# Cross-attention with a gated residual, first batch: banks of the gate products, places of two memory splits, of the query's split and of the weight clusters, and the ragged tile stacked

## The reference

```
mp    = memory @ W_mem.T                       # 1601 x 512
attn  = softmax(x @ mp.T / sqrt(512))          # 512 x 1601
ctx   = attn @ mp                              # 512 x 512
gate  = sigmoid([x, ctx] @ W_gate.T + b_gate)
fused = x + gate * ctx
out   = fused * rsqrt(mean(fused**2) + 1e-6) * norm_w
```

## Time and profile before

| | |
|---|---|
| median of 3 runs | 537.66 us (537.37 to 537.76) |
| the profiled execution | 537.72 us, of which the span is 535.9 us |
| TensorE's granted clock, mean | 0.996 |
| busy, share of the span | PE 98%, DVE 90%, ACT 60%, POOL 32% |
| the chain of waits | PE 93%, DVE 4%, the rest 1% or less each |

### The profile page before, as it was taken

How to read it: one execution, slowest core, us unless ns; L and a number is a source line. 1 busy time by engine, 2 the same in 40 slices (tenths; PEclk the granted TensorE clock), 3 DMA queues, 4 the chain that set the end, 5 groups by cost and what they waited for, 6 DMA issues and landing times.

```text
span 535.9 us, 8824 instructions
## 1 busy us (share of the span) xinstructions
PE 524.8 (98%) x2364; PEld 431.7 (81%) x2364; DVE 482.8 (90%) x797; ACT 323.2 (60%) x614; POOL 172.2 (32%) x129
## 2 busy tenths in 40 slices
PE   8998999999999999999999999999999999999994
PEld 7876888888888888888888888888888888888883
DVE  3799958999799998999989998899979999899967
ACT  4675636676467655686465863666557765558524
POOL 0004610185004740066200950027400573008702
PEclk9999999999999999999999999999999999999998
DMA  9967263511687027840378105870267502401033
GB/s 226 269 122 125 64 102 91 100 40 31 181 164 130 20 59 168 177 81 20 112 149 185 39 20 173 148 144 21 75 153 167 110 20 76 141 31 39 2 117 119
DMA packets 186118, 56.38 MB, mean 105 GB/s; under 512 B 161756, under 2 KB 175592, under 8 KB 186100
## 3 DMA queue, kind: packets, MB, share of 16 engines
q1 hardware_dynamic: 185572, 55.64, 44.7%
q10 hardware_dynamic: 528, 0.52, 0.3%
HBM read 46.15 MB, written 8.39 MB: 102 GB/s over the span
## 4 chain that ended last, share of the span: by engine, by line
PE 93%; DVE 4%; DMA 1%; issue 1%; ACT 1%; SPq 0%; POOLq 0%; POOL 0%; DVEq 0%
PE bank L391 22%; PE bank L393 21%; PE bank L392 21%; PE bank L567 8%; PE bank L568 8%; PE bank L569 8%; PE bank L470 1%; DMA mem_raw<-in_ctx_dram 1%; PE bank L551 1%; PE bank L550 1%; PE bank L603 0%; DVE wg1t_lo L904 0%; DVE p_lo L904 0%; DVE fused L1081 0%; SPq L339 0%
## 5 line engine op out<-in xcount | busy, mean ns | idle before, releaser
L1256 POOL TENSOR_TENSOR psum_rows<-psum_rows,p_tmp 128x512 f32<-128x512 f32 (+1 forms) x88 | 129.6, 1473 | 39.5 <-ACT p_tmp L735 36.1
L904 DVE TENSOR_TENSOR p_lo<-p_tmp,p_hi 128x512 fp32r<-128x512 f32 (+1 forms) x104 | 89.2, 858 | 5.9 <-ACT p_hi L696 5.9
L1267 POOL TENSOR_TENSOR fused<-fused,x_again 128x512 f32<-128x512 f32 x14 | 17.9, 1300 | 219.1 <-DVE fused L1077 219.1
L391 PE MATMUL bank<-q_hi,mt_hi 128*128 128x512 f32 (+1 forms) x208 | 81.9, 394 | 0.0
L393 PE MATMUL bank<-q_hi,mt_lo 128*128 128x512 f32 (+1 forms) x208 | 81.3, 391 | 0.0
L392 PE MATMUL bank<-q_lo,mt_hi 128*128 128x512 f32 (+1 forms) x208 | 81.2, 390 | 0.0
L735 ACT ACTIVATE p_tmp<-s 128x512 f32<-128x512 f32 (+1 forms) x104 | 64.4, 626 | 27.6 <-DVE s L968 26.5
L567 PE MATMUL bank<-p_hi,mem_hi 128*128 128x512 f32 (+1 forms) x196 | 76.4, 390 | 0.0
L568 PE MATMUL bank<-p_lo,mem_hi 128*128 128x512 f32 (+1 forms) x196 | 76.3, 390 | 0.0
L569 PE MATMUL bank<-p_hi,mem_lo 128*128 128x512 f32 (+1 forms) x196 | 76.3, 389 | 0.0
L696 ACT ACTIVATE s<-bank 128x512 f32<-128x512 f32 (+1 forms) x104 | 62.0, 596 | 19.1 <-PE bank L393 18.7
(11 more groups left out here) (105 smaller groups left out, 1024.7 us busy)
## 6 DMA issues: line engine op xcount, KB each, us to landing
mem_raw<-in_ctx_dram SPq DMA_DIRECT2D x48, 256.0 KB, 3.0
mem_blocks<-in_ctx_dram SPq DMA_DIRECT2D x64, 136.0 KB
x_again<-in_x_dram SPq DMA_DIRECT2D x32, 256.0 KB, 2.8
out_dram<-fused SPq DMA_DIRECT2D x32, 256.0 KB, 2.1
x_raw<-in_x_dram SPq DMA_DIRECT2D x112, 64.0 KB, 2.0
mem_blocks<-in_ctx_dram SPq DMA_DIRECT2D x56, 64.0 KB, 2.0
x_raw<-in_x_dram SPq DMA_DIRECT2D x4, 256.0 KB, 4.9
gate<-in_L_xattn_W_gate_dram SPq DMA_DIRECT2D x2, 512.0 KB, 5.9
```

The source lines that it names most:

```text
L391: nc.tensor.matmul(dst, a_hi, b_hi, start=(start and i == 0), stop=False)
L904: return nc.vector.tensor_tensor(dst, src, hi.bitcast(F32), ALU.subtract)
L1256: nc.gpsimd.tensor_tensor(psum_rows[0:r, :], a, p_tmp[0:r, t % TMP_RING, :], ALU.add).then_inc(p_added, 1)
```

## The change

All of it is in the first batch. Its four gate products use banks 2, 4, 5, 2, and only the fourth waits, for the first's `add_bias`. The WG2T clusters come after tiles 7, 8, 10, 11. DVE's low parts of pairs 4, 5 and 6 are made at t = 4, 6 and 7 of the softmax loop (ACT's high parts stay where they were). ACT makes p_hi of tile 12 first, then mt_hi, then the query's high part; DVE makes mt_lo before q_lo. The ragged tile is stacked as in the other batches: `stack_last_tile(0)` stands in SP's list between the memory loads of batch 1 and the loop.

```diff
-        GX_BANKS = (0, 1, 2, 4)
+        GX_BANKS, FIRST_GX_BANKS = (0, 1, 2, 4), (2, 4, 5, 2)
-            return bank[QX_BANKS[j % 2] if first else GX_BANKS[j]]
+            return bank[(FIRST_GX_BANKS if first else GX_BANKS)[j]]
-        WG2T_AT = [7, 8, 9, 10]
+        WG2T_AT = [7, 8, 10, 11]
+        FIRST_SPLITS = {4: [4], 6: [5], 7: [6]}
@@ SP, before the loop
                 load_mem_again(1, p)
+            stack_last_tile(0)
             with sp.Fori(1, B - 1) as b:
@@ PE, gate_x, first batch
-                    elif j >= 2:
-                        pe.wait_ge(gx_done, NT * b + j - 1)
+                    elif j == 3:
+                        pe.wait_ge(gx_done, NT * b + 1)
@@ PE, weighted_last_tile
-                pe.wait_ge(stacked, 64 * b)
+                pe.wait_ge(stacked, 64 * (b + 1))
@@ PE, iteration
-                    if first or t < MT - 1:
+                    if t < MT - 1:
                         weighted(b, t)
@@ ACT, iteration, first batch's loop
-                        if not last and t == 12:
-                            q_hi_part(b + 1, 0)
-                            q_hi_part(b + 1, 1)
@@ ACT, iteration, every batch but the last, behind the loop
-                if first:
+                if not last:
                     mt_hi_part(b + 1, 0)
                     mt_hi_part(b + 1, 1)
+                    q_hi_part(b + 1, 0)
+                    q_hi_part(b + 1, 1)
@@ DVE, iteration, scores' phase
-                    for q in (SPLIT_BY_SCORES if p < MP - 1 or first else {}).get(p, []):
+                    for q in (SPLIT_BY_SCORES if p < MP - 1 else {}).get(p, []):
                         mem_lo_part(b, q)
@@ DVE, iteration, first batch's softmax loop
-                        for q in SPLIT_BY_SOFTMAX.get(t, []):
+                        for q in FIRST_SPLITS.get(t, []):
                             mem_lo_part(b, q)
@@ DVE, iteration, behind the loop
-                    q_lo_part(b + 1, 0)
-                    q_lo_part(b + 1, 1)
                     if first:
                         mt_lo_part(b + 1, 0)
                         mt_lo_part(b + 1, 1)
+                    q_lo_part(b + 1, 0)
+                    q_lo_part(b + 1, 1)
```

## The result

The changed kernel takes 540.31 us (median of 5, 539.89 to 540.89) against 537.67 (537.37 to 538.48): ratio 1.0048, 95% interval 1.0035 to 1.0062. The direction was forecast, 539.0 was too low and 540.3 lies outside the range. The profiled execution took 540.48 us, its span is 538.7.

What follows compares the result with a forecast made beforehand. PE (98% busy) bounds, with DVE nearly full and bounding tile 9. Tile 9 starting 1.75 us later, less 0.46 for the stacked ragged tile, gives +1.3 us: 539.0, with 8 in 10 from 536.1 to 539.7.

Steps and rivals of the forecast that it cites:

- WG2T's clusters: Ahead of the loop: two clusters wait behind the copy of tile 11's score, so PE resumes 0.15 us later.
- Banks: First batch's gate products: no product waits for its bank; they end at 54.6 instead of 56.95.
- VectorE's lead at tile 9: Softmax loop: DVE is 0.85 us ahead of PE at tile 9; what PE gains beyond that, DVE must gain too.
- The meetings: Softmax loop, t = 4, 6, 7: mem_lo held up by POOL's adds, costing 1.40, 1.37 and 1.42 us; net +2.4 at shift 10.
- The rival without meetings: Softmax loop: POOL's adds not in mem_lo's way, PE starts tile 9 at 68.2, total 536.2; chance 0.21.
- The rival of PE alone: First batch: PE alone bounds, so the whole 2.3 + 0.46 us gain arrives, 534.9; chance 0.04.
- Ragged tile: First batch's tile 12: four matmuls for six save 0.46 us; PE wants it 5.5 after p_lo, copies not late.
- late copies: Ragged tile: stacked copies land 1 to 2 us later than PE wants them, 540 to 541; chance 0.07.
- The step that failed: Ahead of the loop: without two mem_lo (1.20 us) column_max starts at 37.46 and everything after comes 1.05 earlier.
- A further meeting: Softmax loop, shift 10 to p_lo of tile 9: none expected; one would end that p_lo at 71.6 instead of 70.8.

Runs made afterwards that it cites:

- e4: Kernel before with only the banks of the first batch's gate products changed (2, 4, 5, 2): 537.01 us, ratio 0.9986.
- e2: Changed kernel with POOL's adds of the first batch over 32 columns instead of 512, its softmax sums left incomplete: 535.55 us, ratio 0.9959.
- e12: Kernel before with POOL's adds of the first batch over 32 columns instead of 512, its softmax sums left incomplete: 537.19 us, ratio 0.9988.
- e3: Changed kernel with each of the three mem_lo behind its step's shift and ahead of p_lo, split of x after p_lo there: 537.66 us, ratio 0.9995.
- e6: Kernel before with only the three low-part splits moved into the softmax loop (t = 4, 6, 7): 540.35 us, ratio 1.0044.
- e7: Changed kernel, VectorE's loop reordered around POOL's adds: two swaps, pair 4 behind its shift, pairs 5 and 6 at t = 10, memory transposes last, rows wait moved: 537.43 us.
- e13: Changed kernel with 16 more one-column memsets at the start of VectorE's list, one profile: 539.74 us.
- e14: Changed kernel with a one-column memset between the last running maximum and column_max, one profile: 540.40 us.
- e10: Kernel of e7 with mem_lo of pairs 5 and 6 at t = 11 and p_lo of tile 9 ahead of the split of x: 535.73 us, ratio 0.9961.
- e8: Changed kernel with the splits back, V's first low part ahead of p_lo of tile 0 and second add_bias ahead of p_lo of tile 2: 536.53 us, ratio 0.9972.
- e5: Changed kernel with VectorE's wait for the rows of bias and norm moved from ahead of column_max to behind spread_max: 540.29 us.
- e9: Changed kernel with column_max's wait for s_copied dropped, in every batch: 540.02 us.

## Why the prediction was right in its mechanism and wrong in its size

- **WG2T's clusters:** PE resumes 0.15 later by the sum; its idle time grew from 0.71 to 0.87. Right.
- **Banks:** no wait for the third or fourth product, `weighted` at 54.86 where 54.6 was forecast. Right. Alone (e4) the banks bring 0.8 us, about VectorE's lead at tile 9.
- **The meetings:** mem_lo 1.46 and 1.45 us for a forecast of some 1.45, and POOL ahead of pair 6. Right, shown by e2 with e12, by e3 and by e6. That POOL goes ahead of pair 6 was in part luck: the forecast took it from one case, and in e7 the mem_lo went first. The rival without meetings (536.2) didn't come true; with thin adds (e2, 535.55) the kernel comes near it. The rival of PE alone is excluded by TensorE's waits for p_lo here and in e4.
- **Ragged tile:** p_lo of tile 12 ended at 76.49 and PE took the stacked tile at 81.59, 5.10 later, without a wait. Four matmuls took 0.93 us, where six took 1.39. Right, and no late copies. The remark that before the change the last mt_lo was done just ahead of the scores at 80.11 was misread: both mt_lo together ran from 79.15 to 80.42. Nothing in the sum hangs on it.
- **The step that failed** is the one ahead of the loop: "so with the 0.15 it starts at 37.46, and everything after it ... comes 1.05 earlier". It counted the 1.20 us of the two mem_lo as gained in full and put nothing for what their absence would lay open. `column_max` started at 38.25 and WG1T's low parts came 0.25 earlier, not 1.05. Of the missing 0.79, 0.64 is the gap ahead of `column_max`: 0.56 idle, and the 0.08 by which an instruction otherwise starts ahead of the end of the last (37.01 + 0.60 = 37.61 was its place). e13 and e14 show that this gap reaches batch 1's scores. The other 0.15 is the start of the execution, in which the first load of x landed later. What causes the idle time stays open.
- **A further meeting** at tile 8, which the sum left out and only its upper bound held: POOL's add there took 2.00 us and p_lo 0.94 instead of 0.66, 0.27 on the path. Why that add took 2.00 and not 1.61 stays open.

The sum of the profiled executions: 1.3 forecast, 0.64 for the gap, 0.27 for the meeting and 0.05 that is spread out are 2.26, which the change owns; with 0.15 for the start, batch 1's scores come 2.41 later (82.52 against 80.11). A wait of 0.40 for x_again in the tail makes it 2.8, and the executions differ by 2.76. The medians differ by 2.64. Whether the wait for x_again belongs to the change is open: seven of the ten profiles with the three splits in the loop have it (0.40 to 0.79 us), and none of the six others. The forecast's range ended too low because I gave the time before `column_max` no bound, although no row showed it uncovered.

## What to carry to other kernels

When a second engine is nearly as full as the bounding one, find the last point where the bound waits for it (here tile 9, a lead of 0.85 us) and price every move by what it does to that point, not by what it frees elsewhere. Where VectorE reads two SBUF operands while GpSimd adds, the place of an instruction within the step decides whether it costs 0.6 to 0.8 or 1.4 us (mem_lo of pair 4 in e10, in e3 and in the changed kernel). The first meetings can be read off the trace before anything is built; behind them the phases move, and e7 and e8 missed their forecasts by that. An instruction that covers nothing useful may still cover an idle time, so bound what appears when a cover is taken off.

## What the runs showed of the hardware

- Each VectorE subtraction of 128x512 that met an add in the rows of the changed kernel (two mem_lo, p_lo of tile 8) ended 0.55 us after the add did, and took 0.94 to 1.46 us instead of 0.67. The Trainium skill (SBUF — State Buffer, "Who interferes with whom") has the rule of one holding the port for its whole instruction; these rows agree. The same page's about 115 ns until the blocked one resumes ("A bandwidth-pool intuition that's wrong (but worth ruling out)") would, by an estimate, put the end 0.79 after the add's; that isn't seen.
- When an add was issued while a subtraction ran and another one stood next in VectorE's list, either could go first: the add in the changed kernel (pair 6, 0.40 us alone, took 1.51), the mem_lo in e7 (0.67, and the add took 2.20). What decides is open.
- VectorE stood idle for 0.54 to 0.57 us at one place of its list, for none of the two waits that were moved or dropped (e5, e9); 16 more instructions ahead of it made this 0.14 (e13), one beside it 0.09 (e14).
